# A fused attention and RWKV kernel: the order of work in its five-stage rounds redone

## The chip, the cores and the metric

The kernel runs on one core of one Trainium2 chip. All data is float32. The metric is the device time of one launch in microseconds. The kernel before has a median of 2171.43 us over three runs (2171.19 to 2175.91).

## The reference

Two layers follow each other over 8 batches of 256 tokens of 512 features. The first is a transformer block with self attention, cross attention and a feed-forward of width 2048. The second is a recurrent (RWKV) block. The change touches the feed-forward of the first layer and the whole second layer, which the kernel runs together:

```python
x = x + gelu(ln(x, ln3) @ w1 + b1) @ w2 + b2            # end of the first layer

xa = _ln(x, ln1_w, ln1_b)
sx = previous_token(xa) - xa
xxx = tanh((xa + sx * maa_x) @ maa_w1)                   # five groups of 32
xm = xa[:, :, None] + sx[:, :, None] * (maa_stack + xxx @ maa_w2)
xk, xw, xv, xr, xg = five parts of xm
w = exp(-exp(time_decay + tanh(xw @ td_w1) @ td_w2))
r, k, v, g = xr @ Wr.T, xk @ Wk.T, xv @ Wv.T, silu(xg @ Wg.T)
def step(s, rkvw):                                       # over 256 tokens, 32 heads of 16 x 16
    a = k_t[..., :, None] * v_t[..., None, :]
    out = einsum('bhi,bhij->bhj', r_t, u * a + s)
    s = a + w_t[..., :, None] * s
og = normalized per head(out) * gn_w + gn_b
x1 = x + og * g @ Wo.T
xc = _ln(x1, ln2_w, ln2_b)                               # then xk2, xr2 as above
out = x1 + sigmoid(xr2 @ Wfr.T) * (square(relu(xk2 @ Wfk.T)) @ Wfv.T)
```

## The kernel before

`attention_block` does the attention of all batches and the feed-forward of the first. `recurrent_block` does the rest as a pipeline over batches. Its five stages are `l` (layer norm and turning ahead of the feed-forward), `f` (feed-forward), `a` (token shift, mixing, the projections k, w, v, r, g and the first scan steps), `s` (the other scan steps, the normalization per head, `Wo`, the second layer norm) and `d` (channel mixing and output). One round works on up to five batches, one in each stage. `pipeline` issues 10 rounds: `lfa`, `lfas`, four times `lfasd`, `fasd`, `asd`, `sd`, `d`.

Each engine has its own `body`, in which the order of the work in a round is written out by hand. Nothing is scheduled by a tool: an instruction waits on a semaphore for its inputs, and everything behind it on its engine waits with it. SP issues nearly all loads and stores, ACT issues the stores of k, w, v and r.

What the prediction's steps touch:

- PE: `ff1` (L1735, tiles of the first feed-forward product), `ff2` (L1745, tiles of the second), `project_T` (L1768, one tile per half of the output, used for k, v, r, g and `Wfk`), `by_halves` (L1813: `td2`, the decay; `mix4`), `mix_pair` (L1801), `turn` (L1758: `xaT`, `xcT` and `hT3`), `by_group` (L1787: `dev`, the deviation from the mean of a head, then `var`; `bonus`), `add_rows` (L1828, row sums of one scan step into the bank `YS`).
- DVE: `step` (L1987 product k times v, L1998 two scans, L2005 product with r, which lets the row sums of the step start), `shift` (L2015) and `take_ff2` (L2051).
- ACT: `gelu` (L2221), `take` (L2194 copies a projection, L2197 stores it), `take_rows` (L2214 copies four row sums to `osum`), `take_ln` (L2185), `take_hidden` (L2231).
- POOL: L1686 adds `bv` to `o`; L1660 adds `xaT` to a mixed tile (`add_xa`); L1679 makes `sx`.

The scan of one batch has 8 steps: steps 0 to 2 in its `a` round and 3 to 7 in its `s` round. After step 7 the row sums leave PE by a detour: ACT copies them to `osum`, SP stores `osum` to DRAM in four transfers (`store_scan`, L1517), SP loads them back in another layout as `o` (L1589), POOL adds `bv`, and PE computes `dev` from it. The v that the scan needs makes a detour too: ACT copies and stores it (`v_all`), SP loads parts of it, each head's rows to four partitions, as `vs` (L1478). SP's part of this in a round is:

```python
store_scan(s); load_shared("Wg", (a, "v", 1)); load s0
wait o_out;  load o;   wait x3_out; load xr
wait kwvr_out["v"]; load_part(a, 0); load_part(a, 1)
wait kwvr_out["r"]; load rs; next_ff(3); ...
```

The feed-forward and the hidden turn of stage `l` share two PSUM banks. `F_TILES` lists who uses them in which order; tile n lies in bank n % 2, and a tile's first matmul waits until the tile two places ahead has been emptied. `f1` and `hT3` tiles are emptied by ACT, `f2` tiles by DVE.

## Time and profile before

| | |
|---|---|
| median of the runs | 2171.43 us |
| the profiled execution | 2168.41 us, of which its span 2166.7 us |
| granted TensorE clock, mean | 0.945 |
| busy | PE 88%, DVE 66%, ACT 40%, POOL 23% of the span |
| the recurrent block | from about 862 us to the end |
| PE busy in 1200:1800 | 183.83 + 187.88 + 191.09 = 562.8 of 600 us |
| one `lfasd` round | about 153.5 us |

The profile is of one execution of the whole program. It gives the start and length of each instruction, the idle time before it and what ended it, and for a transfer the time from issue to landing. Times are from the span's start. In names, buffer numbers are left out: `b_f_bank` is either bank of the feed-forward, `b_c_bank` holds the tiles of stages `s` and `d`, `b_a_bank` those of `a`.

### The profile page before, as it was taken

What the parts mean: (1) busy time and instruction counts of PE and PEld (TensorE: products, weight loads), DVE (VectorE), ACT (ScalarE), POOL (GpSimd) and SP (SyncE); (2) the same over time, 40 slices, a digit from 0 to 9 for tenths busy, and PEclk for the clock granted to TensorE, in tenths of its full rate; (3) what the DMA queues carried; (4) which work ended last, traced back from release to release, by engine and by line L of the source; (5) the groups of instructions that cost most, each with busy time, mean ns of one, the idle gap of its engine ahead of it and who ended that gap; (6) DMA issues with size and microseconds to landing.
All of it is one profiled execution on the core that took longest, in us unless ns stands there. A gap on an engine that the chain in (4) does not pass through costs nothing.

```text
span 2166.7 us, 28694 instructions
## 1 busy us (share of the span) xinstructions
PE 1916.8 (88%) x11012; PEld 1313.0 (61%) x11012; DVE 1435.2 (66%) x2431; ACT 868.2 (40%) x2022; POOL 495.7 (23%) x242
## 2 busy tenths in 40 slices
PE   5789999999999997897899899899899899987626
PEld 4566666666666664665657656656667656655313
DVE  3366667666766442268679679679678777786852
ACT  2466666666666743212332322422332322312111
POOL 1233334333343321202102202212112111112000
PEclk9799999999999998998999999999999999997868
DMA  7000010000001123454644544644645636434220
GB/s 206 25 1 25 11 35 23 13 25 11 28 18 63 40 75 101 160 189 148 195 146 161 189 163 149 205 156 151 197 130 175 195 114 207 166 116 128 77 97 29
DMA packets 156399, 235.29 MB, mean 109 GB/s; under 512 B 25240, under 2 KB 73112, under 8 KB 156264
## 3 DMA queue, kind: packets, MB, share of 16 engines
q1 hardware_dynamic: 139368, 216.67, 31.0%
q10 hardware_dynamic: 16896, 16.80, 2.3%
q8 instruction: 88, 1.44, 0.3%
q14 instruction: 47, 0.39, 0.1%
HBM read 191.48 MB, written 41.96 MB: 108 GB/s over the span
## 4 chain that ended last, share of the span: by engine, by line
PE 38%; DVE 13%; DMA 3%; issue 2%; ACT 1%; POOL 1%; SPq 1%; ACTq 0%; POOLq 0%; DVEq 0%
PE b_f_bank L1735 7%; PE b_f_bank L1745 7%; PE b_a_bank L1768 7%; PE b_c_bank L1778 6%; DVE b_ring L1998 5%; DVE b_ring L1987 3%; PE b_c_bank L1768 2%; DMA b_o<-b_o_all 2%; PE b_c_bank L1787 2%; PE b_y_bank L1828 2%; PE b_a_bank L1801 2%; DVE b_ring L2005 1%; PE b_a_bank L1863 1%; DMA b_o_all<-b_osum 1%; POOL b_o L1686 1%
## 5 line engine op out<-in xcount | busy, mean ns | idle before, releaser
L401 POOL TENSOR_TENSOR a_prob<-a_prob,a_rowinv 128x1024 f32<-128x1024 f32 x128 | 242.3, 1893 | 510.8 <-DVE a_rowinv L854 510.8
L1086 ACT ACTIVATE a_prob<-a_score,a_low 128x256 f32<-128x256 f32 x512 | 253.6, 498 | 227.6 <-DVE a_low L846 227.6
L1998 DVE TENSOR_TENSOR_SCAN b_ring<-b_ws,b_ring 128x1028 f32<-128x1028 f32 x128 | 324.3, 2575 | 3.0
L1735 PE MATMUL b_f_bank<-k_hT_early,k_w_early 128*128 128x256 f32 x896 | 212.9, 392 | 0.9 <-ACTq L57 0.9
L1745 PE MATMUL b_f_bank<-k_w_early 128*128 128x512 f32 x448 | 208.3, 614 | 0.1
L846 DVE CUSTOM_DVE_ANT_0 a_score<-a_score,a_fill 128x256 f32<-128x256 f32 x512 | 196.7, 448 | 4.8 <-DVE a_score L833 0.2
L1987 DVE TENSOR_TENSOR b_ring<-b_ks,b_vs 128x2048 f32<-128x2048 f32 x64 | 178.1, 2782 | 30.4 <-issue 29.7
L1735 PEld LDWEIGHTS b_f_bank<-k_hT_early,k_w_early 128*128 128x128 f32 x896 | 173.6, 197 | 38.6 <-issue 15.2
L1660 POOL TENSOR_TENSOR b_mixed<-b_mixed,b_xaT 128x1024 f32<-128x1024 f32 x40 | 109.3, 2750 | 329.8 <-DVE b_mixed L2015 329.8
L833 DVE SCALAR_TENSOR_TENSOR a_score<-a_S,a_mask 128x1024 f32<-128x1024 f32 x128 | 150.8, 1220 | 49.2 <-PE a_S L595 49.2
L1768 PE MATMUL b_a_bank<-b_mixed,b_shared 128*128 128x256 f32 x768 | 172.8, 384 | 4.8 <-DMA b_shared<-in_Wk_dram 3.5
L826 DVE TENSOR_SCALAR a_ctxT<-a_O,a_vec 128x256 f32<-128x256 f32 x64 | 31.0, 484 | 210.0 <-PE a_O L625 210.0
L1768 PEld LDWEIGHTS b_a_bank<-b_mixed,b_shared 128*128 128x128 f32 x768 | 147.9, 193 | 26.4 <-issue 4.1
L2005 DVE TENSOR_TENSOR b_ring<-b_ring,b_rs 128x2048 f32<-128x2048 f32 x64 | 151.8, 2373 | 2.2
L1745 PEld LDWEIGHTS b_f_bank<-k_w_early 128*128 128x128 f32 x448 | 86.7, 197 | 100.1 <-issue 99.4
L609 PEld LDWEIGHTS a_S<-k_ident,a_prob 128*128 128x128 f32 x1024 | 121.7, 146 | 30.6 <-issue 15.3
L609 PE MATMUL a_S<-k_ident,a_prob 128*128 128x128 f32 x1024 | 129.1, 282 | 9.9 <-DVE a_score L833 9.9
L1098 ACT ACTIVATE a_probT<-a_S 128x1024 f32<-128x1024 f32 x128 | 128.6, 1007 | 11.0 <-PE a_S L609 11.0
L2221 ACT ACTIVATE k_w_early<-b_f_bank,k_b_col 128x256 f32<-128x256 f32 x112 | 47.0, 471 | 194.3 <-PE b_f_bank L1735 194.3
L496 PE MATMUL a_G<-k_hT_early,k_w_early 128*128 128x256 f32 x512 | 118.9, 387 | 6.0 <-DMA k_w_early<-in_w_qkv_dram 4.9
L2015 DVE SCALAR_TENSOR_TENSOR b_mixed<-b_a_bank,k_vec_b,b_sx 128x256 f32<-128x256 f32 x160 | 66.3, 477 | 78.7 <-PE b_a_bank L1813 48.1
L496 PEld LDWEIGHTS a_G<-k_hT_early,k_w_early 128*128 128x128 f32 x512 | 96.6, 193 | 22.6 <-DMA k_w_early<-in_w_qkv_dram 5.3
(163 smaller groups left out, 2943.4 us busy)
## 6 DMA issues: line engine op xcount, KB each, us to landing
k_w_early<-in_w_dram SPq DMA_DIRECT2D x64, 1024.0 KB, 5.3
b_vs<-b_v_all SPq DMA_DIRECT2D x32, 512.0 KB, 5.0
b_shared<-in_Wv_dram SPq DMA_DIRECT2D x8, 1024.0 KB, 6.6
b_shared<-in_Wk_dram SPq DMA_DIRECT2D x8, 1024.0 KB, 5.3
b_shared<-in_Wg_dram SPq DMA_DIRECT2D x8, 1024.0 KB, 5.8
b_shared<-in_Wo_dram SPq DMA_DIRECT2D x8, 1024.0 KB, 5.9
b_shared<-in_Wfk_dram SPq DMA_DIRECT2D x8, 1024.0 KB, 5.9
b_shared<-in_Wfv_dram SPq DMA_DIRECT2D x8, 1024.0 KB, 5.1
```

The costliest lines, as they stand in the source:

```text
L401: nc.gpsimd.tensor_tensor(two, two, inv.to_broadcast([P, 2 * TT, SEQ]), ALU.mult)\
L496: last = nc.tensor.matmul(bank[:, m * SEQ:(m + 1) * SEQ], w[:, c, col + m * P:col + (m + 1) * P], actT[:, c, :], start=(c == 0), stop=(c = ...
L609: last = nc.tensor.transpose(S[:, j, k * SEQ + a * P:k * SEQ + (a + 1) * P], prob[:, HPG * (g % 2) + j, a * SEQ + k * P:a * SEQ + (k + 1) ...
L833: last = nc.vector.scalar_tensor_tensor(out=score[:, 2 * pair:2 * pair + 2, :], in0=S[:, 2 * pair:2 * pair + 2, :], scalar=-SCORE_SCALE, i ...
L846: last = nc.vector.tensor_tensor_reduce(sc, sc, fill[:, at, a * SEQ:(a + 1) * SEQ], 1.0, 3.0e38, ALU.add, ALU.min, low[:, HPG * g + j, a:a ...
L1086: last = nc.scalar.activation(prob[:, slot, a * SEQ:(a + 1) * SEQ], score[:, j, a * SEQ:(a + 1) * SEQ], ACT.Exp, bias=low[:, head, a:a + 1 ...
L1735: last = nc.tensor.matmul(bank[:, m * SEQ:(m + 1) * SEQ], w1[:, cg, col_:col_ + P], hTf[:, cg, :], start=(cg == 0), stop=(cg == CG - 1))
L1745: last = nc.tensor.matmul(bank[:, :], f1T(quarter, cg)[:, at * P:(at + 1) * P], w2[:, cg, :], start=(cg == 0), stop=(cg == CG - 1))
L1768: last = nc.tensor.matmul(tile(name, k)[:, m * SEQ:(m + 1) * SEQ], w[:, c, (2 * k + m) * P:(2 * k + m + 1) * P], act[:, c, :], start=(c == ...
L1987: nc.vector.tensor_tensor(slot[:, :, :, 1:SEQ + 1], ks[:, :, :].unsqueeze(1).to_broadcast([P, JCOLS, IROWS, SEQ]), vs[:, u // 2 % 2, u % 2 ...
L1998: last = nc.vector.tensor_tensor_scan(x_, flat(ws[:, :, :]), x_, 0.0, ALU.mult, ALU.add)
L2005: nc.vector.tensor_tensor(x_, x_, rs[:, :, :].unsqueeze(1).to_broadcast([P, JCOLS, IROWS, SEQ]), ALU.mult).then_inc(weighed.sem, 1)
```

## The change

No work is added or removed; every engine does the same operations in another order. (1) PE does `ff2` tile 1 ahead of `td2`. (2) The row sums of step 7 move between the two halves of v. On ACT the copy of the row sums moves ahead of the copies of v. (3) `ff1` tile 5 and its gelu move ahead of `dev`. The first half of g takes its place between `dev` and `var`. (4) `ff1` tile 7 goes ahead of turning `xcT`, the hidden turn `hT3` follows directly, and then come `ff2` tiles 4 to 7. `F_TILES` gives `hT3` the places 12 and 13. On ACT gelu 7 goes ahead of the copies of `xcT`. (5) SP waits for the store of v and loads `vs` parts 0 and 1 ahead of `o` and `xr`. (6) In rounds that have no `d` (the first two), `ff1` 1 goes ahead of turning `xaT` and `ff1` 2 behind it. (7) In the round without `f` (`asd`), DVE does step 6 behind the two `shift_pair` calls.

```diff
-        F_TILES = [F1, F1, F1, F1, F2, F2, F1, F1, F2, F2, F1, F1, F2, F2, HT3, HT3, F2, F2]
+        F_TILES = [F1, F1, F1, F1, F2, F2, F1, F1, F2, F2, F1, F1, HT3, HT3, F2, F2, F2, F2]
...
                         .then_inc(s0_in.sem, 16)
+                    sp.wait_ge(kwvr_out["v"].sem, kwvr_out["v"].at(a, 1))
+                    alone(sp)
+                    load_part(a, 0)
+                    load_part(a, 1)
                 if s is not None:
                     sp.wait_ge(o_out.sem, o_out.at(s, 1))
...
                 if a is not None:
-                    sp.wait_ge(kwvr_out["v"].sem, kwvr_out["v"].at(a, 1))
-                    alone(sp)
-                    load_part(a, 0)
-                    load_part(a, 1)
                     sp.wait_ge(kwvr_out["r"].sem, kwvr_out["r"].at(a, 1))
...
                 if f is not None:
                     ff1(t, f, 0)
+                    if d is None:
+                        ff1(t, f, 1)
...
                     turn(a, "xaT", xa)
+                if f is not None and d is None:
+                    ff1(t, f, 2)
...
                     mix_pair(a, (2, 3), 1)
+                if f is not None:
+                    ff2(t, f, 1)
+                if a is not None:
                     pe.wait_ge(*emptied(a, "td1", 0))
                     by_halves(a, "td2", ...
-                if f is not None:
-                    ff2(t, f, 1)
...
                     pe.wait_ge(mix_made.sem, mix_made.at(a, 3))
-                    project_T(a, "v", loaded("Wv", a), mixed[:, 0, :, :])
+                    project_T(a, "v", loaded("Wv", a), mixed[:, 0, :, :], (0,))
                 if s is not None:
                     add_rows(s, 7)
                 if a is not None:
+                    project_T(a, "v", W["Wv"], mixed[:, 0, :, :], (1,))
...
+                if f is not None:
+                    ff1(t, f, 5)
                 if s is not None:
                     pe.wait_ge(o_made.sem, o_made.at(s, 1))
                     by_group(s, "dev", lambda cg: dev_head[:, :], lambda cg: o[:, cg, :])
-                if f is not None:
-                    ff1(t, f, 5)
+                if a is not None:
+                    pe.wait_ge(mix_made.sem, mix_made.at(a, 5))
+                    project_T(a, "g", loaded("Wg", a), mixed[:, 0, :, :], (0,))
...
-                    project_T(a, "g", loaded("Wg", a), mixed[:, 0, :, :])
+                    project_T(a, "g", W["Wg"], mixed[:, 0, :, :], (1,))
...
+                if f is not None:
+                    ff1(t, f, 7)
                 if s is not None:
                     pe.wait_ge(c_h.sem, c_h.at(s, 1))
                     turn(s, "xcT", ...
-                if f is not None:
-                    ff1(t, f, 7)
-                    ff2(t, f, 4)
-                    ff2(t, f, 5)
                 if l is not None:
                     pe.wait_ge(l_h.sem, l_h.at(l, 1))
                     turn(l, "hT3", xa, t)
                 if f is not None:
-                    ff2(t, f, 6)
-                    ff2(t, f, 7)
+                    for i in range(4, 8):
+                        ff2(t, f, i)
...
                 if s is not None:
                     step(s, 5)
-                    step(s, 6)
+                    if f is not None or a is None:
+                        step(s, 6)
...
                 if s is not None:
+                    if f is None and a is not None:
+                        step(s, 6)
                     step(s, 7)
...
                     gelu(f, 4)
+                if s is not None:
+                    take_rows(s, 1)
                 if a is not None:
                     take(a, "v", vT, v_dram)
-                if s is not None:
-                    take_rows(s, 1)
```

The rest of the diff moves ACT's gelus 1, 2, 5 and 7 to match.

In full rounds, PE's order around `dev` was this (L1813 with `b_tdt` is `td2`, L1768 with `b_shared` is v and, behind `var`, g):

```order
L1813 MATMUL b_a_bank<-b_tdt,b_td_w 128x256 x4
L1745 MATMUL b_f_bank<-k_w_early 128x512 x4
L1828 MATMUL b_y_bank<-b_ring,k_same_quad 32x128 x16
L1735 MATMUL b_f_bank<-k_hT_early,k_w_early 128x256 x8
L1768 MATMUL b_a_bank<-b_mixed,b_shared 128x256 x16
L1828 MATMUL b_y_bank<-b_ring,k_same_quad 32x128 x16
L1768 MATMUL b_a_bank<-b_mixed,b_Wr 128x256 x16
L1813 MATMUL b_a_bank<-b_t,b_maa_w 128x256 x4
L1787 MATMUL b_c_bank<-b_o,k_dev_head 128x256 x4
L1735 MATMUL b_f_bank<-k_hT_early,k_w_early 128x256 x8
L1787 MATMUL b_c_bank<-b_sq,k_mean_head 128x256 x4
L1768 MATMUL b_a_bank<-b_mixed,b_shared 128x256 x16
```

With the change:

```order
L1745 MATMUL b_f_bank<-k_w_early 128x512 x4
L1813 MATMUL b_a_bank<-b_tdt,b_td_w 128x256 x4
L1828 MATMUL b_y_bank<-b_ring,k_same_quad 32x128 x16
L1735 MATMUL b_f_bank<-k_hT_early,k_w_early 128x256 x8
L1768 MATMUL b_a_bank<-b_mixed,b_shared 128x256 x8
L1828 MATMUL b_y_bank<-b_ring,k_same_quad 32x128 x16
L1768 MATMUL b_a_bank<-b_mixed,b_shared 128x256 x8
L1768 MATMUL b_a_bank<-b_mixed,b_Wr 128x256 x16
L1813 MATMUL b_a_bank<-b_t,b_maa_w 128x256 x4
L1735 MATMUL b_f_bank<-k_hT_early,k_w_early 128x256 x8
```

The row sums (`b_y_bank`) stand between two halves of 8 matmuls of v, and a group of `ff1` stands ahead of `dev`.

SP's queue in a full round from the store of the row sums on was this (`b_vs` is v for the scan, `b_o` the row sums on their way back):

```order
L1517 DMA b_o_all<-b_osum 256x1x128 x4
L1508 DMA b_shared<-in_Wg_dram 128x4x512
L1583 DMA b_s<-in_enc_dram 128x64
L1589 DMA b_o<-b_o_all 128x4x256
L1594 DMA b_xr<-x_all 128x2x512
L1478 DMA b_vs<-b_v_all 128x1x1024 x2
L1483 DMA b_rs<-b_r_all 128x1024
```

With the change:

```order
L1517 DMA b_o_all<-b_osum 256x1x128 x4
L1508 DMA b_shared<-in_Wg_dram 128x4x512
L1583 DMA b_s<-in_enc_dram 128x64
L1478 DMA b_vs<-b_v_all 128x1x1024 x2
L1593 DMA b_o<-b_o_all 128x4x256
L1598 DMA b_xr<-x_all 128x2x512
L1483 DMA b_rs<-b_r_all 128x1024
```

The two `b_vs` loads stand ahead of `b_o`.

PE's order from the last row sums of a full round to its end was this (L1758 turns: `b_sq` is `xcT`, `b_xa` is `hT3`):

```order
L1828 MATMUL b_y_bank<-b_ring,k_same_quad 32x128 x16
L1758 MATMUL b_c_bank<-k_ident,b_sq 128x128 x8
L1735 MATMUL b_f_bank<-k_hT_early,k_w_early 128x256 x8
L1745 MATMUL b_f_bank<-k_w_early 128x512 x8
L1758 MATMUL b_f_bank<-k_ident,b_xa 128x128 x8
L1745 MATMUL b_f_bank<-k_w_early 128x512 x8
L1735 MATMUL b_f_bank<-k_hT_early,k_w_early 128x256 x8
```

With the change:

```order
L1828 MATMUL b_y_bank<-b_ring,k_same_quad 32x128 x16
L1735 MATMUL b_f_bank<-k_hT_early,k_w_early 128x256 x8
L1758 MATMUL b_c_bank<-k_ident,b_sq 128x128 x8
L1758 MATMUL b_f_bank<-k_ident,b_xa 128x128 x8
L1745 MATMUL b_f_bank<-k_w_early 128x512 x16
L1735 MATMUL b_f_bank<-k_hT_early,k_w_early 128x256 x8
```

The two turns stand together, behind `ff1` 7 and ahead of all four `ff2` tiles.

## Rows read from the trace of the kernel before

**Rows 1.** The page's first line
```profile
span 2166.7 us, 28694 instructions
```

**Rows 2.** Waits 1000:1910: engine line <- releaser: total, times, longest (us)
```profile
PE b_c_bank L1787 <- POOL b_o L1686: 36.0, 6, 6.9
```

**Rows 3.** PE's timeline, third round with row sums: start, us, line, op, count [idle before]
```profile
1352.49 1.13 PE L1813 MATMUL b_a_bank<-b_tdt,b_td_w 64*128 64x256 f32 x8 [1.05 <-DVE b_mixed L2015]
...
1361.76 7.07 PE L1768 MATMUL b_a_bank<-b_mixed,b_shared 128*128 128x256 f32 x32
1368.76 1.08 PE L1828 MATMUL b_y_bank<-b_ring,k_same_quad 128*32 128x128 f32 x32
...
1384.01 3.78 PE L1787 MATMUL b_c_bank<-b_o,k_dev_head 128*128 128x256 f32 x8 [6.00 <-POOL b_o L1686]
```

**Rows 4.** SP's queue in the same stretch: start, us of issuing, line, transfer
```profile
1370.62 2.57 SPq L1517 DMA_DIRECT2D b_o_all<-b_osum  x4
1373.30 0.55 SPq L1508 DMA_DIRECT2D b_shared<-in_Wg_dram  x1
...
1375.19 0.38 SPq L1589 DMA_DIRECT2D b_o<-b_o_all  x1
...
1376.21 1.25 SPq L1478 DMA_DIRECT2D b_vs<-b_v_all  x2
```

**Rows 5.** Transfers issued in 1366:1394: KB each, us from issue to landing
```profile
b_v_all<-b_vT ACTq DMA_DIRECT2D x1, 512.0 KB, 3.8
...
b_o<-b_o_all SPq DMA_DIRECT2D x1, 512.0 KB, 6.3
```

**Rows 6.** DVE's timeline, the last product of step 7
```profile
1363.23 2.29 DVE L2005 TENSOR_TENSOR b_ring<-b_ring,b_rs 128x2048 f32<-128x2048 f32 x1
```

**Rows 7.** Timelines of SP, then ACT: the load of `Wo`, the stores of k and v
```profile
1339.37 0.37 SPq L1508 DMA_DIRECT2D b_shared<-in_Wo_dram  x1
...
1340.00 0.37 ACTq L2197 DMA_DIRECT2D b_k_all<-b_kT  x1
...
1369.54 0.37 ACTq L2197 DMA_DIRECT2D b_v_all<-b_vT  x1
```

**Rows 8.** Transfers issued in 1337:1357
```profile
b_k_all<-b_kT ACTq DMA_DIRECT2D x1, 512.0 KB, 6.7
```

**Rows 9.** Transfers issued in 1325:1345
```profile
b_bv<-b_bv_all SPq DMA_DIRECT2D x1, 512.0 KB, 8.3
```

**Rows 10.** End of that round, PE's timeline, then ACT's
```profile
1421.97 3.62 PE L1735 MATMUL b_f_bank<-k_hT_early,k_w_early 128*128 128x256 f32 x16
...
1435.15 0.67 PE L1758 MATMUL b_f_bank<-k_ident,b_xa 128*128 128x128 f32 x4 [2.25 <-DVE k_enc_early L2051]
...
1421.74 1.93 ACT L2185 ACTIVATE b_xcT<-b_c_bank,k_vec_b 128x256 f32<-128x256 f32 x4 [0.25 <-PE b_c_bank L1758]
...
1432.93 1.02 ACT L2231 ACTIVATE k_hT_early<-b_f_bank,k_vec_b 128x256 f32<-128x256 f32 x2 [6.46 <-PE b_f_bank L1758]
```

**Rows 11.** PE's timeline, first two rounds of the block
```profile
876.38 5.14 PE L1863 MATMUL b_a_bank<-b_z,b_maa_w 128*128 128x256 f32 x16 [5.72 <-DVE b_z L2068]
...
1004.88 5.73 PE L1863 MATMUL b_a_bank<-b_z,b_maa_w 128*128 128x256 f32 x16 [12.13 <-DVE b_z L2068]
...
1043.82 1.13 PE L1801 MATMUL b_a_bank<-b_t,b_maa_w 32*128 32x256 f32 x8
```

**Rows 12.** DVE's timeline, second round: the first half of the third mix pair
```profile
1038.96 1.65 DVE L2015 SCALAR_TENSOR_TENSOR b_mixed<-b_a_bank,k_vec_b,b_sx 128x256 f32<-128x256 f32 x4
```

**Rows 13.** Round without a feed-forward batch: PE's timeline, then SP's
```profile
1971.47 1.08 PE L1828 MATMUL b_y_bank<-b_ring,k_same_quad 128*32 128x128 f32 x32 [0.84 <-DVE b_ring L2005]
...
1986.35 3.78 PE L1787 MATMUL b_c_bank<-b_o,k_dev_head 128*128 128x256 f32 x8 [5.63 <-POOL b_o L1686]
...
1978.37 0.38 SPq L1589 DMA_DIRECT2D b_o<-b_o_all  x1
```

**Rows 14.** Transfers issued in 1673:1700
```profile
b_v_all<-b_vT ACTq DMA_DIRECT2D x1, 512.0 KB, 2.9
```

More of the change, by code:

```diff
@@ L1875, in body @@
                     mix_pair(a, (0, 1), 1)
-                if f is not None:
+                if f is not None and d is not None:
                     ff1(t, f, 1)
@@ L1879, in body @@
                     add_rows(s, 4)
-                if f is not None:
+                if f is not None and d is not None:
                     ff1(t, f, 2)
@@ L1922, in body @@
                     by_group(s, "dev", lambda cg: dev_head[:, :], lambda cg: o[:, cg, :])
-                if f is not None:
-                    ff1(t, f, 5)
+                if a is not None:
+                    pe.wait_ge(mix_made.sem, mix_made.at(a, 5))
+                    project_T(a, "g", loaded("Wg", a), mixed[:, 0, :, :], (0,))
                 if s is not None:
@@ L1928, in body @@
                 if a is not None:
-                    pe.wait_ge(mix_made.sem, mix_made.at(a, 5))
-                    project_T(a, "g", loaded("Wg", a), mixed[:, 0, :, :])
+                    project_T(a, "g", W["Wg"], mixed[:, 0, :, :], (1,))
                     pe.wait_ge(rk_made.sem, rk_made.at(a, 1))
@@ L1947, in body @@
                     turn(s, "xcT", sq[:, :, :].rearrange("p c t -> p (c t)").rearrange("p (a n) -> p a n", a=TT))
-                if f is not None:
-                    ff1(t, f, 7)
-                    ff2(t, f, 4)
-                    ff2(t, f, 5)
                 if l is not None:
@@ L2241, in body @@
                     gelu(f, 0)
+                    if d is None:
+                        gelu(f, 1)
                 if d is not None:
@@ L2250, in body @@
                     take_ln(a, "xaT", xaT, "m_ln1_w", "m_ln1_b", 1)
+                if f is not None and d is None:
+                    gelu(f, 2)
                 if s is not None:
@@ L2264, in body @@
                     take_rows(s, 0)
-                if f is not None:
+                if f is not None and d is not None:
                     gelu(f, 1)
@@ L2268, in body @@
                     begin(s, 6)
-                if f is not None:
+                if f is not None and d is not None:
                     gelu(f, 2)
@@ L2308, in body @@
                     begin(a, 1)
+                if f is not None:
+                    gelu(f, 5)
                 if s is not None:
@@ L2316, in body @@
                             .then_inc(empty_sem("dev"), 1)
-                if f is not None:
-                    gelu(f, 5)
-                if s is not None:
                     act.wait_ge(*filled(s, "var", 1))
@@ L2347, in body @@
                     begin(a, 3)
+                if f is not None:
+                    gelu(f, 7)
                 if s is not None:
                     take_ln(s, "xcT", xcT, "m_ln2_w", "m_ln2_b", 0)
-                if f is not None:
-                    gelu(f, 7)
                 if l is not None:
```

## The prediction

> **What bounds the kernel now.** I read the busy table by stretch first: in a full round PE is busy for some 94% of the time, so only what stops PE counts there. Then the list of waits over the rounds 1000:1910 us. Its largest wait of PE is the one of `dev` (L1787) for POOL's add on `o`: 36.0 us in 6 rounds, 6.0 each [rows 2]. PE's timeline shows where it stands: PE does v, the row sums of step 7, r and `mix4`, and then idles for 6.00 us [rows 3]. The chain of waits goes from there back through POOL, the load of `o` and SP's stores to the row sums. So the end of a round is set by a detour through DRAM that starts at the row sums of step 7 and ends at `dev`. Two more idle times are in view: 1.05 us ahead of `td2` [rows 3] and 2.25 us in the middle of `hT3` [rows 10]. After the last round with a feed-forward batch the waits of DVE's steps and of this detour set the end.
>
> All times below are those of the round at 1291:1444. Call its row sums of step 7 A = 1368.76 [rows 3].
>
> **Parts 2 and 3, the detour on PE and ACT.** Step 7's product ends at 1363.23 + 2.29 = 1365.52 on DVE [rows 6]. The first half of v ends at 1361.76 + 3.5 = 1365.3 [rows 3]; with `ff2` 1 ahead of `td2` (part 1) the 1.05 us wait ahead of it is covered and v is done at 1364.2, but the row sums then wait for step 7. So the 1.05 us are given back here. The row sums start at 1365.6 instead of 1368.76: 3.2 us earlier. Their copy goes ahead of those of v on ACT, so the four stores start at 1370.62 - 3.2 = 1367.4 and are issued in 2.57 us, until 1370.0 [rows 4]. The second half of v ends at 1365.6 + 1.0 + 3.45 = 1370.05, 0.3 us behind the 1369.77 of before, and PE is through `mix4` at 1378.0 + 0.3 = 1378.3 (before: 1384.01 - 6.00 = 1378.01) [rows 3]. `ff1` 5, 3.5 us by its neighbour [rows 10], then covers to 1381.8. If the load of `o` moved up by 3.2 us as well, `dev` would be ready at 1380.8, no wait would be left, and a round would gain 6.0 us, some 36 in all.
>
> **Part 5, the detour on SP.** It does not move up, because SP's queue now waits for the store of v first. The last half of v ends 1.3 us later than before (1370.05 against 1368.76), so its store is issued at 1369.54 + 1.3 = 1370.8 [rows 7]. `Wg`, whose load waits for the same tile, is issued at 1370.1, 0.7 us ahead of it; before it was 3.8 us behind it (1373.30) [rows 4]. What the store takes beside such a load is not in view for v. From below: it took 3.8 us beside the row sums' stores [rows 5] and 2.9 in another round [rows 14]. From the other side: the store of k, the same size and form, is issued at 1340.00, 0.63 us behind the 1 MB of `Wo` at 1339.37 [rows 7], and lands after 6.7 us [rows 8]. I take 6.7, since that is the situation of v after the change nearly to the tenth.
>
> So v has landed at 1377.5. The two `vs` loads take 1.25 us to issue [rows 4], and `o` is issued at 1378.85 instead of 1375.19: 3.7 us later. That the row sums have long been stored doesn't help. `o` took 6.3 us with `Wg` 1.9 us ahead of it [rows 4, 5]. Now it has the two `vs` loads 1.3 us ahead and the store of r beside it from its start. The bounds are 6.3 and the 8.3 us of the `bv` load, which follows a 1 MB load and a store [rows 9]; I take 6.8, near the lower end, as again 1 MB is ahead. `dev` followed the landing of `o` by 1384.01 - 1375.19 - 6.3 = 2.5 us. It starts at 1378.85 + 6.8 + 2.5 = 1388.15, 4.1 us later than before, with `ff1` 5 (3.45) already done: the round is 0.7 us longer, and PE still idles for 6.4 us ahead of `dev`. The same holds in all six rounds of rows 2: **+4 us**.
>
> The earlier `vs` lets DVE start step 0 some 2 us sooner. PE never waits for step 0 in a full round, so that is worth nothing. The half of g between `dev` and `var` covers ACT's squares as `ff1` 5 did; it needs `add_xa`, the add on POOL behind the one on `o` and of the same size (under the 2.5 us that lie between the landing of `o` and `dev`), which `dev` covers with its 3.78 [rows 3].
>
> The Trainium skill, DMA: Bandwidth & Descriptors (Anatomy of one DMA; Specifications) gives a transfer a fixed cost of about 2 us, most of it the receipt of the last write, and HBM about 358 GB/s. By that the store of v would land after an estimated 2 + 0.5 MB / 358 GB/s = 3.5 us, and the sum would be some 22 us lower. The two shortest v stores agree (2.9 and 3.8), the k store (6.7) doesn't: the page's Rules for kernel authors say that transfers from two issuers share the same 16 engines packet by packet, and this one has company.
>
> **Part 4, the turns.** `hT3`'s second half waited for DVE's `take_ff2` 5 (2.25 us) [rows 10]. Now it waits for gelu 7, which is done in time. But `ff2` 4 needs the bank that `hT3` 0 filled, and ACT empties that only after gelu 7, the 1.93 us of copying `xcT` and half a `take_hidden` (1.02) [rows 10]. With `ff1` 7 ending at 1421.04 + 3.5 = 1424.5, ACT is through at 1424.6 + 1.0 (gelu 7, two tiles of the size of a `take_hidden`) + 0.1 + 1.93 + 1.02 = 1428.7, while PE is done turning at 1426.3: a wait of 2.4 us for one of 2.25. **0 us**, in five rounds; the bounds are -2.3 (ACT in time) and +1 each.
>
> **Part 6, the first two rounds.** `z` is late by 5.72 us in the first and 12.13 us in the second [rows 11]. `ff1` 1 ahead of the turn delays the first `z` by as much as it fills; `ff1` 2 covers 3.5 us. But both used to cover the mixing behind `z`, which now shows: k waits for a shift (1.65 us) [rows 12] and an add (some 2.5) behind the last mix pair, and I take 2 us as left. In the second round `z` hangs on DVE's step 3 and stays at 1004.88. Everything behind it moves up by 7 us on PE until `mix_pair` (2, 3), 1, which waits for the first pair's shift at 1038.96 + 1.65 = 1040.6 [rows 12] and stood at 1043.82 [rows 11]: 3 us are left. **-5 us**; bounds -8 and -2.
>
> **Part 7 and the `asd` round.** Row sums 7 start when DVE's step 7 ends, at 1971.47 [rows 13], and DVE has the same steps and shifts to do by then, in either order. So putting them between the halves of v gains nothing here, but the second half of v, all done before, now ends at 1971.47 + 1.1 + 3.5 = 1976.1. Store of v at 1976.8, landed at 1983.5, `o` issued at 1984.8 instead of 1978.37 [rows 13], `dev` some 7 us behind its 1986.35. Half a g covers 1 us behind `dev`. **+6 us**, all of which reaches the end, since DVE's next step stands behind the product that waits for this chain. Bounds +2 (v lands in 2.9) and +10.
>
> **Sum.** 4 + 0 - 5 + 6 = +5 us. The profiled execution took 2168.41 us, its span 2166.7 [rows 1]; it would become 2173.4. The median of the runs is 3.0 us above it, so I forecast 2171.43 + 5 = 2176.4 us.
>
> **The rivals.** A measurement of this kernel can tell about 0.2% (4.3 us) from no change.
>
> (A) The store of v lands as its own rows have it, before `Wg` gets in its way. Each microsecond that it lands earlier is worth one in seven rounds, 7 us in all. At 4.7 us the sum is 5 - 14 = -9: 2162 us; at 2.9 it is 2150. The total turns to a gain where v lands under 6.0 us. For it: the row sums' stores are nearly through when v's starts, and ACT's queue is empty. Against it: the k store of every round beside `Wo`. 30%.
>
> (B) The turns do better: ACT empties `hT3`'s bank a microsecond sooner, because DVE's `take_ff2` 5 is out of the way, or `o` finds the engines free and lands in its 6.3. That is 1 us in five or 0.5 us in seven rounds, 2171 to 2173 us: no change. 27%.
>
> (C) The collision is worse: v lands after 8.3 and `o` after 8.3, the `bv` price, and a round costs 3.8 us: +27, 2198 us. A part of it, half as much, is 2187. 10%.
>
> My forecast has 33%.
>
> **Numbers.** Slower by over 0.2%: forecast and (C), 0.43. Within 0.2%: 0.27. Faster by over 0.2%: 0.30. As cases of both signs hold most of the chance: the forecast's own range is 2172 to 2183. The range over the cases goes from 2157, most of (A), to 2189, most of (C).
>
> **What would show it.** In the profile after: the row sums between the v halves 3.2 us earlier; `v_all` landing in 6 to 7 us and `o` issued behind `vs`, 10 us after A and not 6.4; a wait of `dev` for POOL still near 6 us in the full rounds and `dev` 7 us later in `asd`; a wait of `ff2` 4 (L1745) for ACT's `hT_early` of about 2.4 us, and none of `hT3` for DVE. If `dev`'s wait is under 4 us in the full rounds, or the v store lands under 6, the prediction is wrong and the kernel is faster.

## The result, and the profile after

The changed kernel takes 2203.1 us (median of 4 runs, 2201.2 to 2207.6) against 2171.3 for the kernel before: ratio 1.0145, 95% interval 1.0124 to 1.0167. The forecast was 2176.4, its range 2157 to 2189. The sign was right; the size, 5 us forecast for 31.8 measured, was six times too small. The page's first line, against [rows 1]:

```profile
span 2200.1 us, 28694 instructions
```

PE's waits over 1000:1910, against [rows 2]:

```profile
PE b_c_bank L1787 <- POOL b_o L1686: 55.2, 6, 9.6
PE b_f_bank L1745 <- ACT k_hT_early L2240: 10.5, 5, 2.1
PE b_y_bank L1828 <- DVE b_ring L2011: 8.0, 6, 1.3
PE b_a_bank L1867 <- DVE b_z L2074: 6.4, 1, 6.4
```

The wait of `dev` grew from 36.0 to 55.2 us, though `ff1` 5 (3.7 us) now stands ahead of it. The second line is the wait of `ff2` 4 that was forecast at 2.4 us; the third is the row sums standing still between the halves of v.

PE's timeline of the third round, against [rows 3]:

```profile
1361.78 3.62 PE L1768 MATMUL b_a_bank<-b_mixed,b_shared 128*128 128x256 f32 x16
1366.72 1.08 PE L1828 MATMUL b_y_bank<-b_ring,k_same_quad 128*32 128x128 f32 x32 [1.33 <-DVE b_ring L2011]
1367.73 3.72 PE L1768 MATMUL b_a_bank<-b_mixed,b_shared 128*128 128x256 f32 x16
...
1379.35 3.72 PE L1735 MATMUL b_f_bank<-k_hT_early,k_w_early 128*128 128x256 f32 x16
1391.78 3.78 PE L1787 MATMUL b_c_bank<-b_o,k_dev_head 128*128 128x256 f32 x8 [8.70 <-POOL b_o L1686]
1395.89 4.44 PE L1768 MATMUL b_a_bank<-b_mixed,b_shared 128*128 128x256 f32 x16 [0.34 <-POOL b_mixed L1660]
```

The chain that ended last, in the same stretch (start, us, what), says what that wait consists of:

```profile
1366.72 1.08 PE b_y_bank L1828 x32
1367.80 3.67 PE b_a_bank L1768 x16
...
1372.16 6.88 DMA b_v_all<-b_vT
...
1380.42 7.11 DMA b_o<-b_o_all
...
1387.67 4.05 POOL b_o L1686
1391.72 4.13 POOL b_mixed L1660
```

The store of v and the load of `o` now stand one behind the other. SP's queue joins them, against [rows 4]:

```profile
1371.54 0.39 SPq L1508 DMA_DIRECT2D b_shared<-in_Wg_dram  x1
...
1379.11 1.22 SPq L1478 DMA_DIRECT2D b_vs<-b_v_all  x2
1380.42 0.59 SPq L1593 DMA_DIRECT2D b_o<-b_o_all  x1
```

The last two links of the chain are POOL adds of 4.05 and 4.13 us, which took 2.34 and 2.17 before. DVE works on step 0 at the same time, which experiment 3 shows to be the cause for the add on `o`. DVE in this stretch:

```profile
1384.87 2.29 DVE L1993 TENSOR_TENSOR b_ring<-b_ks,b_vs 128x2048 f32<-128x2048 f32 x1 [2.62 <-issue]
1387.29 6.59 DVE L2004 TENSOR_TENSOR_SCAN b_ring<-b_ws,b_ring 128x1028 f32<-128x1028 f32 x2
1393.91 4.07 DVE L2011 TENSOR_TENSOR b_ring<-b_ring,b_rs 128x2048 f32<-128x2048 f32 x1
```

In the kernel before, the add on `o` was over when step 0 began, and it was DVE's first product that took longer (3.75 us instead of 2.29), beside POOL's add for g. That trace already held the price for POOL too: an add of this size took 4.23 us beside the product and the scans of step 7, and 2.17 us where it ran ahead of step 0.

```profile
1354.62 4.23 POOL L1660 TENSOR_TENSOR b_mixed<-b_mixed,b_xaT 128x1024 f32<-128x1024 f32 x1
1381.62 2.34 POOL L1686 TENSOR_TENSOR b_o<-b_o,b_bv 128x1024 f32<-128x1024 f32 x1 [22.76 <-DMA b_o<-b_o_all]
1383.91 2.17 POOL L1660 TENSOR_TENSOR b_mixed<-b_mixed,b_xaT 128x1024 f32<-128x1024 f32 x1
```
```profile
1356.85 6.35 DVE L1998 TENSOR_TENSOR_SCAN b_ring<-b_ws,b_ring 128x1028 f32<-128x1028 f32 x2
1384.48 3.75 DVE L1987 TENSOR_TENSOR b_ring<-b_ks,b_vs 128x2048 f32<-128x2048 f32 x1 [3.66 <-issue]
```

Where the 33.4 us of span come from, by the starts of `dev` in both timelines (the last column is the forecast's 5 us, split at the same points):

| stretch | before | after | difference | forecast |
|---|---|---|---|---|
| span's start to the block's first `ff1` | 863.2 | 860.4 | -2.8 | 0 |
| block start to the first `dev` (its step 7: -3.65) | 213.9 | 217.9 | +4.0 | -0.9 |
| five rounds, `dev` to `dev` | 766.8 | 785.8 | +19.0 | +3.5 |
| last of them to `dev` of `asd` | 142.4 | 152.6 | +10.2 | +3.6 |
| that `dev` to the end | 180.35 | 183.4 | +3.1 | -1.0 |

From step 7's product (start) to `dev` it was 20.8 us before and is 27.4 now in the third round. That one detour, gone through once in the first stretch, five times in the rounds and once in `asd`, is where most of the time went.

### The profile page after: what moved, and what is told of

Its sections match the earlier page's. It is cut to its first block, busy times and chain, and to the rows that moved or that the text cites. A ratio compares the mean times of both kernels' runs of the same rounds, so it can differ in the third digit from the quotient of the medians.

```text
span 2200.1 us, 28694 instructions
## 1 busy us (share of the span) xinstructions
PE 1916.8 (87%) x11012; PEld 1306.9 (59%) x11012; DVE 1445.2 (66%) x2431; ACT 865.2 (39%) x2022; POOL 524.9 (24%) x242
## 4 chain that ended last, share of the span: by engine, by line
PE 37%; DVE 10%; DMA 5%; POOL 3%; ACT 3%; issue 2%; SPq 1%; POOLq 0%; DVEq 0%; ACTq 0%
PE b_f_bank L1745 8%; PE b_c_bank L1778 7%; PE b_f_bank L1735 6%; PE b_a_bank L1768 6%; DVE b_ring L2004 4%; DMA b_v_all<-b_vT 3%; DMA b_o<-b_o_all 3%; PE b_c_bank L1768 2%; DVE b_ring L1993 2%; PE b_y_bank L1828 2%; PE b_a_bank L1801 2%; POOL b_o L1686 1%; DVE b_ring L2011 1%; POOL b_mixed L1660 1%; PE b_a_bank L1867 1%
## 5 line engine op out<-in xcount | busy, mean ns | idle before, releaser
L2004 DVE TENSOR_TENSOR_SCAN b_ring<-b_ws,b_ring 128x1028 f32<-128x1028 f32 x128 | 331.3, 2629 | 3.0
L1745 PE MATMUL b_f_bank<-k_w_early 128*128 128x512 f32 x448 | 203.0, 604 | 10.9 <-ACT k_hT_early L2240 10.9
L1735 PE MATMUL b_f_bank<-k_hT_early,k_w_early 128*128 128x256 f32 x896 | 208.4, 386 | 0.9 <-ACTq L57 0.9
L1660 POOL TENSOR_TENSOR b_mixed<-b_mixed,b_xaT 128x1024 f32<-128x1024 f32 x40 | 123.2, 3098 | 313.0 <-DVE b_mixed L2021 313.0
L1768 PE MATMUL b_a_bank<-b_mixed,b_shared 128*128 128x256 f32 x768 | 186.2, 400 | 11.7 <-issue 4.9
L1735 PEld LDWEIGHTS b_f_bank<-k_hT_early,k_w_early 128*128 128x128 f32 x896 | 168.4, 192 | 38.4 <-issue 17.4
L1993 DVE TENSOR_TENSOR b_ring<-b_ks,b_vs 128x2048 f32<-128x2048 f32 x64 | 169.9, 2655 | 26.0 <-issue 23.7
L1768 PEld LDWEIGHTS b_a_bank<-b_mixed,b_shared 128*128 128x128 f32 x768 | 153.3, 202 | 42.2 <-issue 10.9
L2011 DVE TENSOR_TENSOR b_ring<-b_ring,b_rs 128x2048 f32<-128x2048 f32 x64 | 162.3, 2536 | 2.2
L1828 PE MATMUL b_y_bank<-b_ring,k_same_quad 128*32 128x128 f32 x2048 | 73.5, 287 | 50.5 <-DVE b_ring L2011 50.5
```

The costliest lines, as they stand in the source:

```text
L1735: last = nc.tensor.matmul(bank[:, m * SEQ:(m + 1) * SEQ], w1[:, cg, col_:col_ + P], hTf[:, cg, :], start=(cg == 0), stop=(cg == CG - 1))
L1745: last = nc.tensor.matmul(bank[:, :], f1T(quarter, cg)[:, at * P:(at + 1) * P], w2[:, cg, :], start=(cg == 0), stop=(cg == CG - 1))
L1768: last = nc.tensor.matmul(tile(name, k)[:, m * SEQ:(m + 1) * SEQ], w[:, c, (2 * k + m) * P:(2 * k + m + 1) * P], act[:, c, :], start=(c == ...
L1993: nc.vector.tensor_tensor(slot[:, :, :, 1:SEQ + 1], ks[:, :, :].unsqueeze(1).to_broadcast([P, JCOLS, IROWS, SEQ]), vs[:, u // 2 % 2, u % 2 ...
L2004: last = nc.vector.tensor_tensor_scan(x_, flat(ws[:, :, :]), x_, 0.0, ALU.mult, ALU.add)
L2011: nc.vector.tensor_tensor(x_, x_, rs[:, :, :].unsqueeze(1).to_broadcast([P, JCOLS, IROWS, SEQ]), ALU.mult).then_inc(weighed.sem, 1)
```

## The experiments

Two theories stood at the start: SP's order (part 5) costs the time and TensorE's new order gains some; or TensorE's order (halves, moved tiles) costs it. The second rival was that SP's order costs only where v's store collides with `Wg`.

**1. The change without part 5.**
```
     SP, behind store_scan(s) and s0's load:
-    wait v stored; load_part(a, 0); load_part(a, 1)
     load o; load xr
+    wait v stored; load_part(a, 0); load_part(a, 1)
```


> The changed kernel with SP's loads in the order of before: the two vs loads behind o and xr, so that o's load no longer waits for v's store to land. Theory (SP's order costs the time): the row sums 7 still start where the change put them, about 3 us earlier than before, o is issued about 4.6 us behind o_all as it was before, and with ff1 5 ahead of the deviation (3.62 us) the deviation's wait falls from about 9.2 us to 0-1; VectorE's step 0 starts only behind the POOL add on o, which goes back from 4.05 to about 2.34 us. A round should be 8 to 11 us shorter than with the change, 147 to 150 us instead of 157.2, unless another chain takes over: 2140 to 2165 us, nearest 2150. Rival (TensorE's new order, the halves of v and the moved feed-forward tiles, costs the time): the round stays above 155 us and the time at 2190 us or more.

2132.0 us, ratio to before 0.9813 (0.9796 to 0.983): the theory's side, and 8 us under its range. PE's wait and `dev` in the third round:

```profile
PE b_c_bank L1787 <- POOL b_o L1686: 7.5, 6, 1.5
```
```profile
1367.64 1.99 PE L1787 MATMUL b_c_bank<-b_o,k_dev_head 128*128 128x256 f32 x8 [1.42 <-POOL b_o L1686]
1369.76 3.72 PE L1768 MATMUL b_a_bank<-b_mixed,b_shared 128*128 128x256 f32 x16
```

So everything but part 5 gains 39 us, and part 5 costs 71 on top of it. A round is 146.8 us long. POOL's add on `o` came down to 2.98 us on average and not to 2.34. The cost of 71 us can be added up from the two profiles, to within 3 us: `dev`'s wait in six rounds 55.2 - 7.5 = 47.7; `dev` itself at 1.99 instead of 3.78, 10.7; the half of g behind it at 3.72 instead of 4.44, 4.3; the wait in `asd` 12.49 - 3.94 = 8.6. Together 71.3, where the spans of the two profiles differ by 68.3.

**2. Part 5 alone in the kernel before.**
```
+    wait v stored; load_part(a, 0); load_part(a, 1)
     load o; load xr
-    wait v stored; load_part(a, 0); load_part(a, 1)
```


> The kernel before with SP's new order alone: the vs loads ahead of o. Before, v's store was issued 3.8 us ahead of Wg's load and landed in 3.8 us, so v should be down when SP gets to the vs loads. Theory (SP's order costs much only together with v's store issued beside Wg's load): o is issued 0.5-1 us later for the 1.25 us of issuing, and the POOL add on o may meet VectorE's step 0 (4.05 instead of 2.34 us): +1 to +2.5 us in each of six rounds, 2177 to 2187 us. Rival (SP's order alone is the whole cost): the deviation's wait goes up by 4 us a round, 2195 us or more. Rival (the order is free where v lands early): 2170 to 2174 us.

2202.8 us, 1.0137 (1.012 to 1.0154): the theory fell, and the rival with the full cost held. Here v's store has landed when SP gets to it, as the theory said, but the load of `o` takes 9.8 us instead of 6.1, behind `Wg` and the 1 MB of the `vs` loads. Transfers and wait, over 1000:1910:

```profile
b_v_all<-b_vT ACTq DMA_DIRECT2D x6, 512.0 KB, 2.9
b_o<-b_o_all SPq DMA_DIRECT2D x6, 512.0 KB, 9.8
```
```profile
PE b_c_bank L1787 <- POOL b_o L1686: 65.8, 6, 11.7
```

Part 5 costs 31 us here and 71 in the changed kernel. Read the other way, the rest of the change gains 39 us without part 5 and nothing beside it (2203.1 against 2202.8); experiment 12 shows what eats the gain.

**3. Step 0 kept off POOL's add.**
```
     DVE, ahead of step(a, 0):
+    if s is not None: dve.wait_ge(o_made.sem, o_made.at(s, 1))
```


> The changed kernel, but VectorE starts step 0 of the next tile only when POOL has made o (both halves), so that the two do not run side by side. Theory (the POOL add on o is slowed by VectorE's step 0): the add falls from 4.05 to about 2.34 us, the deviation starts 1.7 us earlier in each of six rounds, and since step 0 is not waited for soon, the time falls by about 8 to 12 us, to 2190-2196 us. Rival (the add is slow for another reason, or VectorE has no slack for a step 0 that starts about 4 us later): the add stays near 4 us or the gain is lost behind it, 2201 us or more.

2192.0 us, 11 below the change, as expected: six rounds of 1.71 us make 10.3. POOL's add on `o` is back at its length before while `o` lands as late as in the change (7.1). The group in the change, then in this kernel:

```profile
L1686 POOL TENSOR_TENSOR b_o<-b_o,b_bv 128x1024 f32<-128x1024 f32 x6 | 24.3, 4053 | 169.1 <-DMA b_o<-b_o_all 169.1
```
```profile
L1686 POOL TENSOR_TENSOR b_o<-b_o,b_bv 128x1024 f32<-128x1024 f32 x6 | 14.0, 2339 | 168.7 <-DMA b_o<-b_o_all 168.7
```

**4. `Wg` moved away from v's store.**
```
-    load_shared("Wg", (a, "v", 1))      # ahead of s0, vs, o, xr
     ... load vs; load o; load xr
+    load_shared("Wg", (a, "v", 1))
```


> The changed kernel with Wg's load moved behind the loads of o and xr, so that v's store has no load beside it. Theory (v's store lands late, 6.9 us, because Wg's load is beside it): it lands in 2.9 to 3.8 us, the vs loads and o are issued 3 to 4 us earlier, the deviation's wait falls from about 9.2 to 5.5-6.5 us, and the time falls by 15 to 24 us, to 2179-2188 us; Wg itself must land before the deviation ends, and should. Rival (the store's landing is long whatever is beside it, as for the 7 us of ring and r loads): landing stays above 6 us, time at 2198 us or more.

2168.1 us, 35 below the change and 11 under the expected range. v's store lands in 2.9 us instead of 7.0, so `Wg` beside it was what made it long:

```profile
b_v_all<-b_vT ACTq DMA_DIRECT2D x6, 512.0 KB, 2.9
b_o<-b_o_all SPq DMA_DIRECT2D x6, 512.0 KB, 7.2
```

`dev`'s wait falls from 55.2 to 26.5 us in six rounds. In the third round it falls by 5.1 us, from 8.70 to 3.62: 3.5 from the landing of v's store (3.41 instead of 6.88) and 1.5 from POOL's add (2.55 instead of 4.05).

**5 to 7. Parts 7, 6 and 4 undone, each in the kernel of experiment 1.** Their edits put back the lines of the diff: `step(s, 6)` ahead of the shift pairs; `ff1` 1 and 2 behind the mix pairs; the old `F_TILES` and the turns between `ff2` tiles.

> The kernel of e1_old_sp (the change with SP's old order) with step 6 of the last round with an attention tile back where it was, ahead of the shift pairs. Read against e1_old_sp (2132.0). Theory (the move of step 6 behind the shift pairs costs the last such round what the prediction gave it): step 6 and the last row sums come 2 to 5 us earlier, 2127 to 2131 us. Rival (the shift pairs are waited for there, which is what the move was good for): 2133 us or more. No difference within 1 us would mean that neither ends last there.

> The kernel of e1_old_sp with ff1 1 and 2 of the rounds without an output tile back behind the mix pairs. Read against e1_old_sp (2132.0). Theory (as the fronts of the traces say: 3.7 us from the block's start to step 7 of the second round): 2135 to 2138 us. Prediction's term: 5 us, 2137. Rival (the gain of the fronts is given back at the next wait): 2131 to 2133 us.

> The kernel of e1_old_sp with the turned tiles xcT and hT3 and their list in the order of before. Read against e1_old_sp (2132.0). Theory (as predicted: a wait of 2.4 us for ScalarE in the place of one of 2.25 us for VectorE, nothing gained): 2130 to 2134 us. Rival (the new order matters once the deviation no longer waits, because the round's tail then has less slack): 2137 us or more.

2133.5, 2137.4 and 2132.2 us against 2132.0. Part 7 is worth nothing that can be told (intervals of the ratios 0.981 to 0.9839 and 0.9796 to 0.983): the theory that it costs 2 to 5 us fell. Part 6 gains 5.4 us (interval of its ratio 0.9828 to 0.9857, which just touches the one of experiment 1). Part 4 is worth 0.

**8. `o` ahead of `Wg`.**
```
-    load_shared("Wg", (a, "v", 1))      # ahead of s0 and o
     load o
+    load_shared("Wg", (a, "v", 1))
     load xr; load vs
```
(in the kernel of experiment 1)


> The kernel of e1_old_sp with Wg's load put behind o's load, ahead of xr. Read against e1_old_sp (2132.0), where o lands in 7.3 us with Wg's 1 MB issued 1.9 us ahead of it and the deviation waits 1.42 us. Theory (o's landing is long because Wg's load is ahead of it): o lands in 4 to 6 us, the deviation's wait goes away in six rounds, Wg still lands before the g half starts, 2122 to 2128 us. Rival (the landing isn't shortened, or Wg is then late for g): 2131 us or more.

2121.9 us, 0.9772 (0.9758 to 0.9787): 2.3% below before, the fastest kernel of this study. `o` lands in 4.4 us and `dev` no longer waits in the six rounds; the longest of PE's waits that are left:

```profile
PE b_f_bank L1747 <- ACT k_hT_early L2242: 10.5, 5, 2.1
PE b_a_bank L1869 <- DVE b_z L2076: 6.9, 2, 6.4
PE b_y_bank L1830 <- DVE b_ring L2013: 6.6, 5, 1.3
```

**9. `ff1` 5 back behind `dev`, in the kernel of experiment 1.**
```
+    wait o_made; by_group(s, "dev", ...)
     ff1(t, f, 5)
-    wait o_made; by_group(s, "dev", ...)
```


> The kernel of e1_old_sp with ff1 5 (3.62 us of TensorE) back behind the deviation, with its step on ScalarE. Read against e1_old_sp (2132.0), where the deviation waits 1.42 us for o. Theory (ff1 5 fills a wait for o that stands there otherwise): the deviation starts no earlier, its wait becomes about 5 us, each of six rounds is 3.6 us longer, and up to 5.5 us if the deviation then runs at 3.8 instead of 2.0 us: 2153 to 2165 us. Rival (the order there is free, since ff1 5 then covers the wait for ScalarE ahead of the variance): 2132 to 2140 us.

2169.4 us (its ten runs spread from 2158.8 to 2173.9): the move is worth 37 us, 6.2 a round, more than either expectation. PE in a later round:

```profile
1686.52 3.78 PE L1787 MATMUL b_c_bank<-b_o,k_dev_head 128*128 128x256 f32 x8 [5.07 <-POOL b_o L1686]
1690.09 4.45 PE L1735 MATMUL b_f_bank<-k_hT_early,k_w_early 128*128 128x256 f32 x16
```

Of the 6.2 us, 3.7 are the wait that `ff1` 5 no longer fills. The rest is that `dev` takes 1.8 us and the tile behind it 0.7 us longer than in experiment 1. The granted clock was 0.50 over this `dev` (the level of 1.2 GHz) and 0.82 on average over the tile behind it; in experiment 1, where `dev` waited 1.42 us, it was 1.00 over both (2.4 GHz).

**10. The wait ahead of `o`, the loads behind it, in the changed kernel.**
```
     wait v stored
-    load_part(a, 0); load_part(a, 1)
     load o; load xr
+    load_part(a, 0); load_part(a, 1)
```


> The changed kernel with SP's wait for v's store left ahead of o, but the two vs loads (1 MB) issued behind o and xr. Read against the change (2203.1) and e1_old_sp (2132.0): it parts the two things that SP's order does. Theory (both count, the wait and the 1 MB that o's load then shares the DMA engines with, and the POOL add that meets VectorE's step 0): o is issued 1.3 us earlier, lands in 4.5 to 6 instead of 7.1 us, the POOL add takes 2.3 to 3.3 instead of 4.05 us, together 3.5 to 5 us in each of seven rounds: 2168 to 2180 us. Rival (the wait for v's store is all of it): 2188 us or more. Rival (the loads ahead of o are all of it): 2150 us or less.

2154.4 us, between the two bounds but under the range. Taken away in this order, 49 of the 71 us of part 5 belong to the two loads ahead of `o` and 22 to SP's wait for v's store. The 49 hold three things that this run doesn't part: the 1.3 us of issuing, the longer landing of `o`, and POOL's add that meets step 0. `o` lands in 4.8 us and POOL's add takes 2.34:

```profile
b_v_all<-b_vT ACTq DMA_DIRECT2D x6, 512.0 KB, 7.0
b_o<-b_o_all SPq DMA_DIRECT2D x6, 512.0 KB, 4.8
```

**11. v in one piece (part 2 undone), in the kernel of experiment 1.**
```
-    project_T(a, "v", ..., (0,));  add_rows(s, 7);  project_T(a, "v", ..., (1,))
+    project_T(a, "v", ...);        add_rows(s, 7)
     (and on ScalarE take v ahead of the row sums)
```


> The kernel of e1_old_sp with v in one piece ahead of the row sums 7, and their order on ScalarE as before. Read against e1_old_sp (2132.0). Theory (each microsecond by which the row sums come earlier is a microsecond of the deviation's wait): the row sums start 2.1 us later, since the 1.33 us that they wait between the halves go away, and so does o; the deviation's wait of 1.42 us grows to about 4.9 us; 2.1 us a round, and up to 3.9 if the deviation falls to half clock: 2145 to 2158 us. Rival (o's landing shortens by as much, because Wg's load, which is issued behind v, keeps its place): 2132 to 2140 us.

2130.7 us, 0.981: the rival held (a little under its 2132), and there is no difference from experiment 1 that can be told. The row sums start later, but v's store is issued well ahead of `Wg` and is down in 3.0 us instead of 8.2, `o` lands in 6.1 instead of 7.8, POOL's add takes 2.34 instead of 2.98. `dev`'s wait is 13.8 instead of 7.5 us in six rounds, and the 6.6 us that PE waited between the halves are gone:

```profile
b_v_all<-b_vT ACTq DMA_DIRECT2D x6, 512.0 KB, 3.0
b_o<-b_o_all SPq DMA_DIRECT2D x6, 512.0 KB, 6.1
```

**12. The same, with SP's new order (the change with v in one piece).**

> The changed kernel (2203.1 us) with v in one piece and ScalarE's order there as before, SP's new order kept. Theory (v's halves put v's store beside Wg's load, which made it land in 7 us, but the vs loads then share the DMA engines with Wg and o instead): v's store lands in 2.9 to 4 us, the vs loads are issued about as soon as SP gets to them, o lands in 9 to 10 us as in e2, the deviation's wait is 7 to 8 instead of 9.2 us; 2187 to 2198 us. Rival (the late store is what made SP's order dear in the change): the wait falls to 4 us or less, 2170 us or less. Rival (nothing changes): 2201 us or more.

2180.4 us, 23 below the change and 7 under the expected range. The mechanism is the expected one (v lands in 3.0, `o` in 9.8, POOL's add 3.03), the gain larger: `dev`'s wait fell by 9.4 us in six rounds and the 8.0 us of waits between the halves of v are gone, 17.4 of the 18.4 by which the spans differ. So beside part 5 the halves of v cost 23 us and the rest of the change gains 22 (2202.8 in experiment 2 against 2180.4); without part 5 the halves cost nothing (experiment 11).

**13. `Wg` behind `o`, alone in the kernel before** (the edit of experiment 8).

> The kernel before with one thing changed: Wg's load behind o's load, ahead of xr. Read against before (2171.9). Theory (Wg's 1 MB in front of o stretches its landing here too): o lands in 4.5 to 5 instead of 6.3 us, the deviation starts 1.5 to 2 us earlier in seven rounds: 2157 to 2163 us. Rival (v's store and o_all take Wg's place and o's landing stays at 6 us or more): 2169 us or more.

2156.7 us, 0.9932 (0.9909 to 0.9955). `o` lands in 3.9 instead of 6.1 us; the wait falls from 36.0 to

```profile
PE b_c_bank L1789 <- POOL b_o L1688: 23.4, 6, 5.1
```

**14. `ff1` 5 ahead of `dev`, alone in the kernel before.**

> The kernel before with one thing changed: ff1 5 ahead of the deviation (its step on ScalarE too). Read against before (2171.4); in e10 the same move was worth 37 us. Theory (g in halves is needed with it, since ff1 5 covered ScalarE's work between deviation and variance): the deviation starts at the same time with a wait of 2.4 us and at 2.0 instead of 3.8 us, but the variance then waits 1.5 to 3 us for ScalarE; net 2 to 4 us in each of six rounds, 2147 to 2160 us. Rival (the move earns its whole price alone, 5 to 6.2 us a round): 2134 to 2141 us. Rival (nothing without the halves): 2168 us or more.

2150.0 us, 0.9904 (0.9883 to 0.9926), in the theory's range: 22 of the 37 us. In a round of it `dev` runs at 3.44 us, and `var` behind it waits for ACT, which half of g covers in the change:

```profile
1526.82 3.44 PE L1787 MATMUL b_c_bank<-b_o,k_dev_head 128*128 128x256 f32 x8 [2.77 <-POOL b_o L1686]
1531.52 1.97 PE L1787 MATMUL b_c_bank<-b_sq,k_mean_head 128*128 128x256 f32 x8 [1.27 <-ACT b_o L2317]
```

**15 and 16. Both of these edits in the kernel before; and v in one piece in the kernel of experiment 8.**

> The kernel before with two things changed: Wg's load behind o's (e13: 2156.7 us) and ff1 5 ahead of the deviation (e15). Theory (o is then ready when TensorE gets there): the deviation's wait falls from 3.9 us in e13 to 0-0.5 us and it runs at full clock, the variance waits for ScalarE as in e15: 2 to 4 us a round less than e13, 2132 to 2145 us. Rival (the two gains cover the same wait and don't add): 2150 us or more.

> The kernel of e8_old_sp_wg_late (2121.9 us) with v in one piece ahead of the row sums 7. Theory: in e8 o is ready 2.7 us before TensorE gets to the deviation; with v whole the row sums end 2.1 us later and TensorE comes 1.33 us earlier, since it doesn't wait between the halves, so the deviation waits 0 to 1 us and a round is 0.3 to 1.3 us shorter: 2114 to 2121 us. Rival (o's landing grows, because Wg's load comes with v's store and o's): the wait is 2 us or more, 2124 us or more.

2160.6 us (the rival's side, and worse than experiment 14) and 2132.4 us (10 worse than experiment 8: the rival's time, but not by its cause, since `o` lands in 3.9 us and `dev` waits for it in two rounds only, 1.7 us together). In both a new wait takes the place of `dev`'s; first the one of 15, then the one of 16:

```profile
PE b_a_bank L1789 <- DVE b_gT L2121: 18.7, 6, 4.6
```
```profile
PE b_a_bank L1789 <- DVE b_gT L2129: 12.4, 6, 4.8
```

`bonus` waits for a product of DVE that stands behind step 0 in DVE's order. In experiment 15 step 0 itself is longer too: in the third round its last product takes 4.26 us instead of 2.29, beside a POOL add (L1694) of 4.31, which takes 2.36 before. That is the meeting of experiment 3 at another place. In experiment 16, with v in one piece and `Wg`, `xr` and `vs` queued behind `o`, step 0 starts late: in a round of it, it starts 5.1 us after `dev` and DVE idles 4.02 us ahead of it, against 1.6 and 2.23 us in a round of experiment 8. That the late landing of `vs` is what holds it was read from the trace, not tested by a run of its own.

Landings are medians and adds are means of six rounds; all are in us.

| kernel | time | v store lands | `o` lands | add on `o` | `dev`'s wait, 6 rounds |
|---|---|---|---|---|---|
| before | 2171 | 2.9 | 6.1 | 2.34 | 36.0 |
| before, SP's new order (2) | 2203 | 2.9 | 9.8 | 2.91 | 65.8 |
| change | 2203 | 7.0 | 7.3 | 4.05 | 55.2 |
| change, v whole (12) | 2180 | 3.0 | 9.8 | 3.03 | 45.8 |
| change, only the wait ahead (10) | 2154 | 7.0 | 4.8 | 2.34 | 21.4 |
| change, SP's old order (1) | 2132 | 8.2 | 7.8 | 2.98 | 7.5 |
| the same, `Wg` behind `o` (8) | 2122 | 3.3 | 4.4 | 2.35 | 0 |

## Why the prediction was wrong, point by point

**Parts 2 and 3 on PE and ACT: half right.** I had put the case without part 5 at 36 us gained; experiment 1 measured 39 (with part 6's 5 in it). That the numbers lie so close is partly luck. The gain hangs on `ff1` 5 ahead of `dev` (37 us, experiment 9), of which 1.8 us a round is a `dev` at full clock that I had not counted, and the halves of v give nothing (experiment 11). I took "3.2 us earlier" as a gain without asking what the halves do to v's own store: it landed in 8.2 us instead of 3.0.

**Part 5, issue of `o`: right.** v's store was taken at 6.7 us and landed in 6.9. `o` was issued at 1380.42, 1.6 us past the forecast's 1378.85, and 1.1 of that is that DVE's step 7, and with it the row sums, stood later in the trace after (1366.72 for a forecast 1365.6).

**Part 5, landing of `o`: the term was too small by a little.** 7.1 for 6.8 in this round.

**Part 5, "`dev` followed the landing of `o` by 2.5 us" and "the earlier `vs` is worth nothing": the step that failed.** The 2.5 us were kept from the trace before, where POOL's add on `o` ended at 1383.96 and step 0 began at 1384.48. The forecast put the landing 4.2 us later and step 0 some 2 us earlier, so by its own numbers the two meet, and it asked only who waits for step 0, not what runs beside it. Measured in the third round, `dev` followed the landing by 4.25 us (1391.78 - 1380.42 - 7.11). Step 0 hardly moved: it began at 1384.87, 0.8 us earlier counted from step 7. It was the add that came 6 us later, into step 0's scans, and took 4.05 us instead of 2.34, as it did in every round (experiment 3 takes that away and gets 11 us back). With 0.5 us at the issue and 0.3 at the landing it makes the detour 6.6 us longer a round instead of 4.1. Behind `dev` the cover that I had counted in full was smaller: the add for g takes 4.13 instead of 2.17, which leaves PE idle for 0.34 us, and the half of g takes 4.44 us for 3.72 at full clock (granted clock 0.83). Together +3.8 a round and not +0.7.

**Rivals.** (C), the worse collision at 2187 to 2198 us, was the nearest and had 10%; it named the landings as the cause, and those were nearly as forecast, so (C) was not right either. (A), v down before `Wg`, did not happen in the change; experiment 4 made it happen and gained 35 us, where (A) had 14 to 26, because POOL's add got shorter with it. (B) was wrong about the turns: they are worth 0 (experiment 7).

**Part 4: right.** The wait of `ff2` 4 is 2.1 us for a forecast 2.4, five times, and undoing the part changes nothing.

**Part 6: right.** 5 us forecast, 5.4 measured (experiment 6). In the second line of the table of stretches it is hidden by the first detour, 7.7 us longer, which lies in the same stretch.

**Part 7 and `asd`: right in kind.** From step 7's product to `dev` it was 12.0 us longer where the forecast had 7. Of the 5 us between, 1.8 are the second half of v, which stood behind a wait of 2.57 us and took 5.41 us at a granted clock of 0.68 where I had 3.5. Nearly all the rest is the landing of `o` (7.24, before 5.46) and POOL's add (4.05, before 2.34). The move of step 6 is worth nothing by itself (experiment 5). Behind that `dev` the forecast had 1 us gained, and 3.1 were lost. The chain of the tail shows where: 32 matmuls of `Wfk` took 10.13 us instead of 8.57 (granted clock 0.70, before 0.83) and the last `var` 3.67 instead of 1.98 (0.53, before 1.00). Their order didn't change; why the clock was lower there stays open.

**The range** ended at 2189, near half of (C), and so left out a case in which a second term goes wrong with the same sign in all seven rounds.

## What to carry to other kernels

When a load is put ahead of another in a queue, price three things: the wait that it brings, the bytes that it puts in front, and what the engine that it feeds will then run beside. In this kernel the wait came to 22 of 71 us and the loads in front to 49, and that holds their bytes, their issuing and the engine beside, which alone made 11 us in the change. Here it paid to let the load that the bound waits for go first and big loads with slack behind it: one moved line (`Wg` behind `o`) was worth 10 to 15 us in both kernels where it was tried alone, but together with `ff1` 5 in the kernel before it gained less than `ff1` 5 alone (experiments 14 and 15), so it needs another look at whoever waits for what it delays. A gain measured alone is no price for the same move beside another: part 5 cost 31 us in one kernel and 71 in the other.
